# Score matmuls issued over four row strips at once instead of two pairs, in both score passes

## What is computed

```python
qkv = x @ w_qkv                      # 16 heads of 8 features
scores = einsum('bhqd,bhkd->bhqk', q, k) / sqrt(8)   # causal, 256 x 256 per head
attn = softmax(where(causal, scores, min))
h = layernorm(x + (attn @ v) @ w_o, g1, b1)
# top 2 of 8 experts by softmax(h @ wg), weights renormalised
h1 = gelu(h @ w1[e] + bb1[e]); y = h1 @ w2[e] + bb2[e]
out = layernorm(h + sum of the two y by their weights, g2, b2)
```

## Time and profile before

| | us |
|---|---|
| median of 3 runs | 1197.24 |
| lowest, highest run | 1195.87, 1200.68 |
| span of the profiled execution | 1192.8 |
| TensorE busy | 1022.4 |
| TensorE weight loads busy | 818.6 |
| VectorE busy | 680.8 |
| ScalarE busy | 670.5 |
| POOL busy | 572.7 |

### The profile page before, as it was taken

How to read it: one execution, slowest core, us unless ns; L and a number is a source line. 1 busy time by engine, 2 the same in 40 slices (tenths; PEclk the granted TensorE clock), 3 DMA queues, 4 the chain that set the end, 5 groups by cost and what they waited for, 6 DMA issues and landing times. The chain is left out here.

```text
span 1192.8 us, 29724 instructions
## 1 busy us (share of the span) xinstructions
PE 1022.4 (86%) x10913; PEld 818.6 (69%) x10913; DVE 680.8 (57%) x2458; ACT 670.5 (56%) x1494; POOL 572.7 (48%) x693
## 2 busy tenths in 40 slices
PE   4799979998989989999989989998999988866470
PEld 2566656886877867686777867687777866766470
DVE  5657665655558835686568835686556723520314
ACT  1243424875758756675667757576666756534240
POOL 2223356235465455555565455554464456542515
PEclk9988877998999989898999979799999979887795
DMA  3394105555555545555556545555556545676562
GB/s 71 86 193 109 37 19 162 167 164 181 154 160 150 172 138 156 147 154 172 149 154 171 165 137 144 153 158 154 160 163 176 170 137 164 202 244 221 212 194 51
DMA packets 117239, 181.01 MB, mean 152 GB/s; under 512 B 13128, under 2 KB 80232, under 8 KB 117096
## 3 DMA queue, kind: packets, MB, share of 16 engines
q1 hardware_dynamic: 108904, 162.32, 47.7%
q0 software_dynamic: 8192, 16.79, 4.9%
HBM read 145.10 MB, written 38.68 MB: 154 GB/s over the span
## 5 line engine op out<-in xcount | busy, mean ns | idle before, releaser
L1173 POOL TENSOR_SCALAR_AFFINE_SELECT probs<-probs 128x512 f32<-128x512 f32 x256 | 182.5, 721 | 262.1 <-ACT probs L706 257.1
L706 ACT ACTIVATE probs<-ps_quad 128x768 f32<-128x768 f32 x256 | 193.7, 807 | 150.3 <-PE ps_quad L527 87.8
L744 ACT ACTIVATE act<-ps_ring,weights 128x128 f32<-128x128 f32 x696 | 191.8, 387 | 96.4 <-PE ps_ring L623 48.0
L874 DVE TENSOR_REDUCE shift_cols<-ps_quad 128x2 f32<-128x512 f32 (+3 forms) x256 | 149.9, 586 | 139.8 <-PE ps_quad L508 125.6
L632 PE MATMUL ps_ring<-weights,act 128*128 128x128 f32 x1392 | 190.8, 285 | 31.1 <-issue 16.4
L632 PEld LDWEIGHTS ps_ring<-weights,act 128*128 128x128 f32 x1392 | 174.5, 198 | 35.1 <-issue 21.6
L623 PE MATMUL ps_ring<-tile_t,weights 128*128 128x128 f32 x1392 | 187.6, 292 | 3.9 <-issue 3.2
L623 PEld LDWEIGHTS ps_ring<-tile_t,weights 128*128 128x128 f32 x1392 | 174.0, 204 | 16.8 <-issue 13.2
L1236 POOL DMA_INDIRECT picked<-sorted_outputs,place x128 | 123.7, 966 | 79.8 <-issue 78.6
L999 DVE TENSOR_TENSOR tile_y<-ps_ring,weights 128x128 f32<-128x128 f32 x174 | 48.8, 287 | 182.2 <-PE ps_ring L632 101.2
L1222 POOL DMA_INDIRECT sorted_rows<-h_rows,place x128 | 124.5, 972 | 53.5 <-issue 34.6
(11 more groups left out here) (165 smaller groups left out, 1531.5 us busy)
## 6 DMA issues: line engine op xcount, KB each, us to landing
weights<-expert_weights SPq DMA_DIRECT2D x174, 578.0 KB
tile_rows<-sorted_rows SPq DMA_DIRECT2D x56, 192.0 KB
sorted_outputs<-tile_y SPq DMA_DIRECT2D x56, 192.0 KB
query_key_parts<-qk SPq DMA_DIRECT2D x32, 256.0 KB, 5.0
k<-query_key_parts SPq DMA_DIRECT2D x64, 64.0 KB
q<-query_key_parts SPq DMA_DIRECT2D x64, 64.0 KB
sorted_rows<-zeros SPq DMA_DIRECT2D x2, 1472.0 KB, 10.7
xs<-in_L_attn_x SPq DMA_DIRECT2D x32, 64.0 KB, 2.3
```

What stands on the lines that cost most here:

```text
L706: sc.activation(probs[:, r % PROBS, 2 * a:2 * a + 2, :], ps_quad[:, 2 * a:2 * a + 2, 0:3 * P], ACT.Exp, scale=HD ** -0.5).then_inc(pair_fr ...
L744: ins = sc.activation(act[:, k % ACTS, f, :], bank(use)[:, f * P:(f + 1) * P], ACT.Gelu_apprx_tanh, bias=weights_of(k)[:, 2 * F + f:2 * F ...
L874: dve.tensor_reduce(shift_cols[:, late, groups], ps_quad[:, groups, 0:split], AX.X, ALU.max)
L1173: pool.affine_select(out=both, in_=both, compare_op=ALU.is_ge, fill=0.0, base=0, pattern=[[0, 2], [0, 2], [1, P]], channel_multiplier=-1). ...
```

## The change

In `scores` the loop over pairs a no longer contains the matmuls of lines 492 to 503. The loop only waits for `pair_free[0]` and then `pair_free[1]`; then the long matmuls of all four strips are issued one behind another, then the short ones of all four. The diagonal matmuls and `pair_full` stay as they were, pair by pair. In `exps` both waits stand ahead too; then come the 128-column matmuls of four strips, then the 256-column ones, where strip 1 raises `pair_full[0]` and strip 3 `pair_full[1]`. The drains on VectorE and ScalarE are unchanged.

```diff
                 for a in range(2):
                     if no:
                         pe.wait_ge(pair_free[a], no)
-                    for j in (2 * a, 2 * a + 1):
-                        rows = slice(32 * j, 32 * j + SLOT)
-                        pe.matmul(ps_quad[:, j, 0:split],
...
-                    for j in (2 * a, 2 * a + 1):
-                        rows = slice(32 * j, 32 * j + SLOT)
-                        pe.matmul(ps_quad[:, j, split:9 * SLOT],
...
+                for j in range(GROUPS):
+                    rows = slice(32 * j, 32 * j + SLOT)
+                    pe.matmul(ps_quad[:, j, 0:split],
...
+                for j in range(GROUPS):
+                    rows = slice(32 * j, 32 * j + SLOT)
+                    pe.matmul(ps_quad[:, j, split:9 * SLOT],
...
                 for a in range(2):
                     pe.wait_ge(pair_free[a], QUAD_NO["exps", n, j])
-                    for i in (2 * a, 2 * a + 1):
...
-                    for i in (2 * a, 2 * a + 1):
...
-                    mm.then_inc(pair_full[a], 1)
+                for i in range(4):
+                    rows = slice(32 * i, 32 * i + SLOT)
+                    pe.matmul(ps_quad[:, i, 0:P], k4[rows, par, j, at + P:at + S], q4s[rows, n % 2, j, P:S],
+                              start=True, stop=True, tile_position=(32 * i, 0))
+                for i in range(4):
+                    rows = slice(32 * i, 32 * i + SLOT)
+                    mm = pe.matmul(ps_quad[:, i, P:3 * P], k4[rows, par, j, at:at + P], q4s[rows, n % 2, j, :],
+                                   start=True, stop=True, tile_position=(32 * i, 0))
+                    if i % 2:
+                        mm.then_inc(pair_full[i // 2], 1)
```

More of the change, by code:

```diff
@@ L491, in scores @@
                         pe.wait_ge(pair_free[a], no)
-                    for j in (2 * a, 2 * a + 1):
-                        rows = slice(32 * j, 32 * j + SLOT)
-                        pe.matmul(ps_quad[:, j, 0:split],
-                                  q_heads[rows, n % 2, late, :, :].rearrange("p h q -> p (h q)"),
-                                  qk[rows, m % 2, 1, at:at + split],
-                                  start=True, stop=True, tile_position=(32 * j, 0))
-                    for j in (2 * a, 2 * a + 1):
-                        rows = slice(32 * j, 32 * j + SLOT)
-                        pe.matmul(ps_quad[:, j, split:9 * SLOT],
-                                  q_heads[rows, n % 2, soon, :, :].rearrange("p h q -> p (h q)"),
-                                  qk[rows, m % 2, 1, at:at + SLOT * (soon + 1)],
-                                  start=False, stop=True, tile_position=(32 * j, 0), skip_group_check=True)
+                for j in range(GROUPS):
+                    rows = slice(32 * j, 32 * j + SLOT)
+                    pe.matmul(ps_quad[:, j, 0:split],
+                              q_heads[rows, n % 2, late, :, :].rearrange("p h q -> p (h q)"),
+                              qk[rows, m % 2, 1, at:at + split],
+                              start=True, stop=True, tile_position=(32 * j, 0))
+                for j in range(GROUPS):
+                    rows = slice(32 * j, 32 * j + SLOT)
+                    pe.matmul(ps_quad[:, j, split:9 * SLOT],
+                              q_heads[rows, n % 2, soon, :, :].rearrange("p h q -> p (h q)"),
+                              qk[rows, m % 2, 1, at:at + SLOT * (soon + 1)],
+                              start=False, stop=True, tile_position=(32 * j, 0), skip_group_check=True)
                 for a in range(2):
@@ L520, in exps @@
                     pe.wait_ge(pair_free[a], QUAD_NO["exps", n, j])
-                    for i in (2 * a, 2 * a + 1):
-                        rows = slice(32 * i, 32 * i + SLOT)
-                        pe.matmul(ps_quad[:, i, 0:P], k4[rows, par, j, at + P:at + S], q4s[rows, n % 2, j, P:S],
-                                  start=True, stop=True, tile_position=(32 * i, 0))
-                    for i in (2 * a, 2 * a + 1):
-                        rows = slice(32 * i, 32 * i + SLOT)
-                        mm = pe.matmul(ps_quad[:, i, P:3 * P], k4[rows, par, j, at:at + P], q4s[rows, n % 2, j, :],
-                                       start=True, stop=True, tile_position=(32 * i, 0))
-                    mm.then_inc(pair_full[a], 1)
+                for i in range(4):
[8 more added lines that the diff above has]
+                        mm.then_inc(pair_full[i // 2], 1)
             def weigh(n, j):
```

## The result

The changed kernel takes 1248.32 us (median of 4 runs, 1242.92 to 1252.78), the kernel before beside it 1198.44 us. The ratio is 1.0407 [1.0371, 1.0444]: slower, as forecast, but by 50 us where 15 were forecast, and outside the range of 1202 to 1222. The profiled execution has a span of 1241.2 us against 1192.8, 48.4 more.

The account below looks back on a forecast made before the run. TensorE was taken to bound the kernel, waiting in turn with ScalarE and VectorE at ps_quad early on. Span 1192.8 + 13.3 + 1 + 1 = 1208.1, plus 4.4 from span to median: 1212 us, range 1202 to 1222.

Parts of the forecast that it names:

- part 6: Clock term: TensorE idling while it waits may cost mean clock; taken as +1 us, bounds -4 and +9.
- One sign: Expected in the next profile: TensorE's 18.5 us idle before `scores` fills for ScalarE grows by 10 to 20.
- Part 4: `exps` fills: ScalarE's drain of pair 0 loses its early start; 13.3 us, 8.0 from 180 to 980, 5.3 before.
- Part 2: Both pair_free waits ahead of first matmul: taken as 0, with 0 to 0.05 us on half the quads inside +4.
- Part 3: `scores` fills: pair 0 waits for pair 1's release, but quad end and drain start stay as before; priced 0.
- Part 1: Matmul order over four strips: small gains in free quads, small losses in the others; 0, bounds -4 and +4 us.
- Part 5: Other work that waits for ScalarE, `weigh` and later gelus and copies: 0 to 3 us, taken as 1.
- A: Rival, chance 0.14: the loss is swallowed, no change; fills less tight than they look, or shorter low-clock stretches.
- B: Rival, 0.04: faster through strip spacing, last strip's end up 0.03 us on 256 quads, 7.7 us; time 1190.
- D: Rival, 0.15: much slower, 1219 to 1228; mean clock falls 0.01 or more, or second wait costs 0.05 us on most quads.
- C: Rival, 0.02: matmuls start strictly in program order, so the change brings pair 1 forward 0.33 us in 124 quads; 1156 us.
- E: Rival in A's share: pair 0's drain still starts before pair 1 is filled, so no quad changes; 1197 us.

Follow-up runs that it names:

- late drain: The kernel before, but ScalarE waits for both pairs of an `exps` fill before it drains pair 0; 1073.09 us, ratio 1.0168.
- the swap: The changed kernel with the wait for pair 1 ahead of that for pair 0, in both functions; 1076.83 us, 1.0265 to the kernel before.
- `scores` half: The kernel before with the change's matmul order and waits in `scores` only, `exps` as before; 1062.51 us, ratio 1.0122.
- early diagonals: The kernel before with pair 0's diagonal matmuls right behind its other matmuls in every `scores` fill; 1058.87 us, ratio 1.0092.

## Why the prediction was right in sign and wrong in size

**What held.** The changed kernel is slower, through the mechanism that was named: ScalarE's drain starts 1.02 us behind the first matmul of a waited `exps` quad, never before pair 1. The `exps` rows are of eight, but for seven fills of 128 on the first chip, most of which TensorE's stalls pull apart (see below), and one on the second. The clock (part 6) moved by 0.002 in the profiled pair. One sign was missed: idle time before `scores` fills for ScalarE was to grow by 10 to 20 us and grew by 53, since idle time here is no measure of the loss.

**Part 4, the head start: right mechanism, too small.** 13.3 us were summed, the late drain measured 19.7. In the middle 8.0 were forecast and 9.8 measured. In the start 5.3 were forecast and 9.7 measured. The forecast was for the first chip, the measurement is from one of the three on which the kernel before takes 1053 us. The walk took each quad of before by itself, with the slack that it had there. It set the price at "never under 0" and let no quad lose its slack to the delay of the one before it. That this is what the start stretch showed is my reading of the fills' shifts, which do not fall back between quads there; no run separates it.

**Part 2, the second wait: the step that failed most plainly.** It was priced at 0, with a bound of 0.05 us on half the quads inside a 4 us allowance. Measured: 10 us by the swap (1086.7 and 1076.8), and 12 in the kernel before, though on its own that run's interval is 5 to 22 us. The rows from which 0 was drawn were those of a fill that waits for nothing; there an extra wait is passed beside the matmuls still running. On a fill that has been waited for, nothing runs beside it: weight load 0.11 to 0.12 us behind the drain and not 0.05, the matmul 0.14 to 0.15 and not 0.05, and the whole `exps` fill ends 1.08 us behind the drain, not 0.99 as in the swapped kernel. 142 of 255 fills are of that kind after the change: 142 x 0.065 = 9.2 us by the weight loads, 142 x 0.09 = 12.8 by the ends of the fills. The 10 and 12 measured lie between. The count was at hand, since 132 fills were counted as split. The Trainium skill says it in one sentence ("Perfetto Trace Analysis", "Identifying Dependency Chains"): instructions that wait on multiple engines may have semaphore instructions put ahead of them for the additional conditions. The trace agrees. Which wait is put ahead, the last one written, and what it costs, 0.06 us on the weight load and 0.09 on the fill where it is the late one, are this case's records.

**Part 3, `scores` fills at 0: wrong.** The `scores` half alone costs 9 us. The argument looked at the end of the quad and left out the second wait, which is added here too. Where the argument looked it was right: in that run the 41 `scores` fills that had been split end 0.014 us later behind pair 1's start (median), although pair 0's matmuls now stand behind the wait for pair 1. But they end 0.105 us later behind the drain that freed pair 1, so some 0.09 of it is the late wait. 79 `scores` fills of that kernel are waited for, and 79 x 0.09 = 7 us is an estimate of the wait's share in the 9. So part 3 failed by the same step as part 2.

**Part 1, the strips: right.** Forecast 0 with a bound of 4 either way. By the records the change brings 0.013 us on a free fill and costs 0.014 on one that used to be split, under 2 us either way. The 6 us between 1092.6 and 1086.7 are the order of the matmuls against pair by pair behind the same two waits, a kernel that the forecast didn't speak of.

**Part 5** (other work that waits for ScalarE, +1) has no run of its own; it is inside the late drain's 19.7.

So on the experiment chips the sum is: head start 19.7, late wait in an instruction of its own 10. That makes 30; the change costs 32 to 33. The other 3 us or so are what the swapped kernel costs (23.3) beyond the late drain (19.8): it waits for both pairs where the late drain could still start pair 0 of the next fill (the row at 209.55), and it has the four-strip order. The runs don't take these two apart, and by the intervals of the ratios the rest could also be nothing.

**What stays open.** On the first chip the middle stretch lost 30 us, on the others 17. TensorE there stands idle in many places without a wait for anything that the trace shows. Summed over all rows of the waits, 44.7 us before and 70.1 us after are put down to "issue"; in the two traces of the second experiment chip 3.7 and 4.3. One such row of the changed kernel on the first chip:

```profile
639.09 1.19 PE L633 MATMUL ps_ring<-weights,act 128*128 128x128 f32 x4 [1.77 <-issue]
```

That the extra 13 us of the middle are these stalls doesn't come out of the totals: between the two marks this idle time grew by 7 us only (35.7 to 42.7), and behind them by 18 (9.0 to 27.4), where the span lost 3.5. On the second chip it is under 1 us between the marks, before and after. So the stalls can be half of the 13 us; the cause of the rest, why the stalls grow with the change, and why the other chips hardly have them, no run shows. Without the first chip's excess the result would have been about +34, still far over +15, so the steps above failed on their own.

**The rivals.** A (swallowed) fell: every trace shows the loss in the start and in the middle. B (strips, faster) fell: it needed 0.03 us on every fill, and the records give 0.013 on the free ones and -0.014 on the others. D was given two causes; the clock did not fall by 0.01 in the profiled pair (in the other runs it may have), and the second wait had, on most waited fills and at more than the 0.05 us stated (0.065 to 0.09). With D's 0.15 the forecast put too little on the case that terms priced at 0 are not 0. C (strict program order) fell too: a free fill is 0.013 us shorter, not 0.33. In the kernel before, pair 1's first matmuls start 0.03 us behind pair 0's and ahead of pair 0's second ones (all eight L494 records in the row at 552.15, the L500 only at 552.69). The early diagonals show that this has an end: with one more matmul per strip between, pair 1 starts 0.33 us behind. The Trainium skill ("TensorE: Matmul & The Clock Gate", Part 3) has matmuls start and end in program order; neither kernel's records follow it for the starts, and both runs are closer to a limited look-ahead. The semaphores do go in program order: in the earlier trace rows pair 0's diagonal matmuls are recorded as over at 203.73 (the ends of matmuls are modelled in the profile), but `pair_full[0]` rises only at 204.36, 0.04 us before `pair_full[1]`, and VectorE starts 0.02 behind it. So it is in the 45 split `scores` fills of that trace, 0.62 us behind the record's end (median). That is why a diagonal matmul recorded early gave no head start. E (the change does nothing) fell with the timeline.

## What to carry to other kernels

Waits that are merged ahead of a group of instructions cost twice: each part loses its head start, and of two waits ahead of one instruction the one written last becomes an instruction of its own. Price both on each fill that is really waited for, and write first the wait that comes latest. Before you price such an edit at 0 from a fill that waits for nothing, look at one that does.

## What was not expected of the hardware

- A wait in an instruction of its own takes 0.051 us in TensorE's queue. If it is the one that comes late, the fill starts 0.14 to 0.15 us behind the drain's end instead of 0.05, and ends 0.09 us later.
- Pair 1's first matmul starts 0.03 us behind pair 0's with two matmuls per strip between them in program order, and 0.33 us behind with three.
- A matmul can be recorded ahead of its place in the program, but its semaphore rises in its place: 0.62 us (median) behind the record's end in the split `scores` fills of the kernel before.
- The same kernel takes 1198 us in the first measurement and 1053 on three chips. In the middle stretch of the kernel before the clock was 0.92 there and 1.00 on the second of the three, and over the span 44.7 us of TensorE's idle time against 3.7 have no shown cause.
